# First sort's shares, the loads of the FFN, the choice of tokens, and idle products on TensorE in a graph and feed-forward kernel

## What is computed

```python
x = x + _L0_gnn_ref(_layernorm(x), edge_index, W, a_l, a_r)         # graph attention, 4 heads
x = x + _L0_ffn_ref(_layernorm(x)[None], ...)[0]                    # FFN on the chosen half of the nodes
x = x + _L1_gnn_ref(_layernorm(x), src, dst, edge_type_4, ...)      # 4 relations, mean over dst, relu
x = x + _L1_ffn_ref(_layernorm(x)[None], ...)[0]                    # 8 experts, top 2
```

```python
weights = (jnp.einsum('bsd,do->bso', x, wr) + br)[..., 0]
k = max(1, int(CAPACITY * s)); kk = k - 1        # 1561 of 3125
_, idx = jax.lax.top_k(weights, k); sel_idx = idx[:, :kk]
h = jax.nn.gelu(jnp.einsum('bkd,dh->bkh', sel, w1) + b1)
y = (jnp.einsum('bkh,hd->bkd', h, w2) + b2) * w_sel[..., None]
```

## Time and profile before

| | us |
|---|---|
| median of 3 runs (1991.79 to 1993.94) | 1993.55 |
| profiled execution, whole | 1998.76 |
| its span, first to last instruction | 1997.0 |
| PE busy, DVE busy, POOL busy, ACT busy | 1437.6, 1302.2, 1391.3, 569.5 |
| mean granted clock of PE | 0.85 of 2.4 GHz |

### The profile page before, as it was taken

How to read it: one execution, slowest core, us unless ns; L and a number is a source line. 1 busy time by engine, 2 the same in 40 slices (tenths; PEclk the granted TensorE clock), 3 DMA queues, 4 the chain that set the end, 5 groups by cost and what they waited for, 6 DMA issues and landing times.

```text
span 1997.0 us, 22558 instructions
## 1 busy us (share of the span) xinstructions
PE 1437.6 (72%) x6235; PEld 944.4 (47%) x6235; DVE 1302.2 (65%) x2919; ACT 569.5 (29%) x1670; POOL 1391.3 (70%) x1400
## 2 busy tenths in 40 slices
PE   5666267788888887569999967766666776457980
PEld 3333045665565555447775434333333333256870
DVE  6999477788898887475995035445444444666544
ACT  0687211146566663032332311000000000242220
POOL 0788777777777777778875457777777777546771
PEclk9799678889999999779999979889877777557995
DMA  5111034444444444802003573333333333412337
GB/s 92 12 31 28 6 102 108 108 105 118 119 119 118 119 104 119 107 17 62 1 2 83 142 220 105 105 106 105 105 106 106 105 106 104 46 52 72 102 103 213
DMA packets 105960, 183.76 MB, mean 92 GB/s; under 512 B 31722, under 2 KB 70077, under 8 KB 105714
## 3 DMA queue, kind: packets, MB, share of 16 engines
q0 software_dynamic: 56928, 134.61, 27.9%
q1 hardware_dynamic: 47603, 45.16, 8.6%
q10 hardware_dynamic: 1308, 2.56, 0.5%
HBM read 151.56 MB, written 30.39 MB: 91 GB/s over the span
## 4 chain that ended last, share of the span: by engine, by line
POOL 38%; PE 19%; DVE 17%; issue 15%; DMA 9%; DVEq 1%; ACT 1%; SPq 0%; POOLq 0%; ACTq 0%
POOL gath L891 29%; POOL slot_tab L711 8%; PE ps L925 6%; DMA gath<-y_tab,index_b 4%; PE ps L1314 4%; PE ps L1703 2%; DVE hot L1160 2%; DMA gath<-h_tab,index_a 2%; DVE hot L1163 2%; PE ps L1714 2%; DVE gath L964 1%; DVE acc L916 1%; DMA wide<-y_nodes 1%; DVE junk_d L1116 1%; DVE hot_c L637 1%
## 5 line engine op out<-in xcount | busy, mean ns | idle before, releaser
L925 PE MATMUL ps<-gath,hot 128*125 128x260 f32 (+1 forms) x1808 | 615.5, 476 | 297.6 <-DVE gath L964 108.5
L925 PEld LDWEIGHTS ps<-gath,hot 128*125 128x125 f32 x1808 | 354.8, 222 | 518.0 <-DMA gath<-y_tab,index_b 190.5
L891 POOL DMA_INDIRECT gath<-h_tab,index_a x464 | 447.4, 964 | 141.1 <-issue 136.5
L891 POOL DMA_INDIRECT gath<-y_tab,index_b x440 | 416.1, 946 | 166.9 <-issue 121.5
L916 DVE TENSOR_TENSOR acc<-acc,ps 125x257 f32 (+1 forms) x672 | 284.6, 423 | 330.8 <-PE ps L925 303.7
L666 PE MATMUL ps<-hot_c,pay 125*128 125x440 f16 (+1 forms) x884 | 191.9, 370 | 60.3 <-ACT pay L655 60.3
L711 POOL DMA_INDIRECT slot_tab<-sent_word,sent_to x119 | 150.5, 1265 | 87.7 <-DVE sent_to L473 51.8
L721 POOL DMA_INDIRECT slot_tab_b<-sent_word_b,sent_to_b x136 | 164.7, 1211 | 38.8 <-issue 34.5
L655 ACT ACTIVATE pay<-hot_r,plan_b 125x128 f16<-125x128 f16 x578 | 172.0, 386 | 0.0
L666 PEld LDWEIGHTS ps<-hot_c,pay 125*128 125x128 f16 x884 | 86.2, 101 | 157.3 <-ACT pay L655 77.0
L964 DVE TENSOR_TENSOR gath<-gath,ps 128x1024 f32<-128x1024 f32 x116 | 136.0, 1214 | 0.0
(11 more groups left out here) (330 smaller groups left out, 2033.7 us busy)
## 6 DMA issues: line engine op xcount, KB each, us to landing
y_tab<-ybuf SPq DMA_DIRECT2D x25, 448.0 KB
gath<-h_tab,index_a POOLq DMA_INDIRECT x464, 2.8
gath<-y_tab,index_b POOLq DMA_INDIRECT x440, 2.8
h_tab<-hbuf SPq DMA_DIRECT2D x25, 113.8 KB
xa<-in_x SPq DMA_DIRECT2D x1, 2800.0 KB
xa<-in_x SPq DMA_DIRECT2D x5, 560.0 KB
xn_tab<-acc SPq DMA_DIRECT2D x25, 112.0 KB
out<-xa SPq DMA_DIRECT2D x5, 560.0 KB
```

Source lines behind the costliest of these rows:

```text
L891: p.indirect_dma_start(gath[:, ring(k) + s, 0:width], None, table, bass.IndirectOffsetOnAxis(ap=index[g][:, col:col + 1], axis=0)).then_in ...
L925: ins = t.matmul(ps[0:NP, 4 + q % 2, 0:width], hot[:, s, :], gath[:, s, 0:width], start=(e == 0), stop=(e == n - 1))
```

## The change

Six things, named in the order of the program:

1. A_STEPS is 19 instead of 18, so SENT is 102 instead of 119.
2. In ffn_sync the loads wait for every second group from 18 on: x in groups 18 to 26, w1 in 28 to 34, w2 in 36 to 42. For that w1_s, w2_s, hid, rel_s and w_turned lie elsewhere in SBUF.
3. ffn_vector scales and norms at once, then waits for the weights and takes the dots. The rank counts are gone. The choice is a search over the bits of the float score in CHOICE: 7, 7, 7, 7 and 3 bits, of which each partition tries one value and counts over the whole row; PE sums the partitions' votes. PE does this at eight places of its own order (CHOICE_AT: set, part, block or tile).
4. stay_warm puts products of the identity with itself on PE, whose results nobody reads: 20 before the FFN's turns, one behind each column of the last three relation groups, 3 for each of 15 tiles in routing, 24 and 14 around the placing of nodes.
5. The relation norms (routing) go in two groups, tiles 0 to 14 and 15 to 24, behind all 25 sums; DVE norms the second group itself.
6. ACT loads its gelu table before it waits for the weights.

```diff
-A_STEPS = 18
+A_STEPS = 19
...
+CHOICE = ((7, 24), (7, 17), (7, 10), (7, 3), (3, 0))
+
+CHOICE_AT = ((1, "up", 2), (1, "up", 6), (2, "up", 1), (2, "up", 4), (2, "up", 7), (2, "down", 1), (2, "down", 3), (3, "up", 2))
...
+    def stay_warm(t, n, bank):
+        for _ in range(n):
+            t.matmul(ps[:, bank, 384:512], ident[:, :], ident[:, :], start=True, stop=True, skip_group_check=True)
...
-        s.wait_ge(planned, 2)
+        s.wait_ge(words_ready, 2)
...
+        phase = iter(range(B_PHASE + 2, GROUPS, 2))
+        beside = lambda: s.wait_ge(added["a"], QUADS * next(phase) + 2)
         for i in range(SETS):
-            s.wait_ge(added["a"], QUADS * (B_PHASE + 2 + 5 * i) + 2)
+            beside()
...
-            s.wait_ge(added["a"], QUADS * (B_END + q) + 2)
+            beside()
             s.dma_start(w1_s[:, :, q * D:(q + 1) * D], matrix(w1)[:, :, q * D:(q + 1) * D]).then_inc(ffn_in, 16)
...
-            s.wait_ge(added["a"], QUADS * (B_END + 4 + q) + 2)
+            beside()
             s.dma_start(w2_s[:, 2 * q:2 * q + 2, :], matrix(w2)[:, 2 * q:2 * q + 2, :]).then_inc(ffn_in, 16)
...
-        s.dma_start(w_all[:, :], bcast(w_tab, NP)).then_inc(wall_in, 16)
+        s.dma_start(w_all[:, :], bcast(w_tab, 128)).then_inc(wall_in, 16)
...
+        for r, (bits, low_bit) in enumerate(CHOICE):
+            v.tensor_tensor(tried[:, :], digits[:, r:r + 1], found[:, :], ALU.bitwise_or).then_inc(vector_step, vn.up())
+            step()
+            v.tensor_scalar(junk, w_all[:, :], tried[:, :].bitcast(F32), None, ALU.is_ge, ALU.add, accum_out=votes[:, :]).then_inc(vector_step, vn.up())
+            step()
+            v.tensor_scalar(chosen[:, :], votes[:, :], wanted[:, 0:1], None, ALU.is_ge).then_inc(wcol_ready, 1)
+            v.wait_ge(wcol_turned, 3 + r)
+            v.tensor_scalar(digit[:, :], ps[:, 7, 256 + r:257 + r], -1.0, float(2 ** low_bit), ALU.add, ALU.mult).then_inc(vector_step, vn.up())
...
+    def choose_tensor(t_eng, place):
+        if place not in CHOICE_AT:
+            return
+        n = CHOICE_AT.index(place)
+        t_eng.wait_ge(wcol_ready, n + 1)
...
+        elif n < 2 + len(CHOICE):
+            tries = 2 ** CHOICE[n - 2][0]
+            ins = t_eng.matmul(ps[:, 7, 254 + n:255 + n], ones[0:tries, :], chosen[0:tries, :], start=True, stop=True)
...
+        ins.then_inc(wcol_turned, 1)
...
-        v.wait_ge(ffn_in, FFN_IN)
-        for t in range(U5):
-            dot(t)
         norm_scale(v, 3, rest)
         v.wait_ge(norm_ready, 3)
...
+        for t in range(U5, 2 * U5):
+            norm(t)
+        v.wait_ge(ffn_in, FFN_IN)
         for t in range(NT):
...
+            if t + 2 * U5 < NT:
+                norm(t + 2 * U5)
+            dot(t)
+        choose_vector(v)
...
+        stay_warm(t_eng, 20, 7)
         for t in range(U5):
             turn(t)
...
+                choose_tensor(t_eng, (i, "up", c))
...
+                choose_tensor(t_eng, (i, "down", u))
...
                 sum_unit(t, "b", k, j, D + 1)
+                if k >= GROUPS_B - 3:
+                    stay_warm(t, 1, 7)
...
+    HALVES = (slice(0, 3 * U5), slice(3 * U5, NT))
...
+        for t in range(8, 23):
+            t_eng.wait_ge(x3_made, t + 1)
+            stay_warm(t_eng, 3, 7)
...
+        stay_warm(t_eng, 24, 5)
         t_eng.wait_ge(er_tile, 2)
...
         ins.then_inc(nodes_made, 1)
+        stay_warm(t_eng, 14, 7)
...
+        for t in range(NT):
+            v.scalar_tensor_tensor(flat(xb, t), acc_cols(t, D), s2[:, t:t + 1], flat(xb, t), ALU.mult, ALU.add).then_inc(third_summed, 1)
+        split = HALVES[1].start
+        measure(0, split)
+        v.wait_ge(vector_step, vn.n)
+        norm_sums(v, HALVES[0])
+        measure(split, split + 2)
+        norm_scale(v, 6, HALVES[0])
+        measure(split + 2, NT)
+        v.wait_ge(vector_step, vn.n)
+        norm_sums(v, HALVES[1])
+        norm_scale(v, 7, HALVES[1])
+        v.wait_ge(norm_ready, 7)
+        for t in range(split, NT):
+            v.tensor_scalar(acc_cols(t, D), flat(xa, t), rstd[:, t:t + 1], nmr[:, t:t + 1], ALU.mult, ALU.add).then_inc(late_normed, 1)
```

More of the change, by code:

```diff
@@ L221, in build @@
     junk_d = mid.tile("junk_d", [NP, D])
-    above = mid.tile("above", [NP, NT, 3])
-    junk = hot[0:NP, :, :].rearrange("p s n -> p (s n)").bitcast(BF16)[:, 0:N]
-    same = mid.tile("same", [NP, NP])
+    digits = mid.tile("digits", [128, len(CHOICE)], I32)
+    found, tried, digit = (mid.tile(n, [128, 1], I32) for n in ("found", "tried", "digit"))
+    votes, chosen, positive, sign, wanted, limit = (mid.tile(n, [128, 1]) for n in ("votes", "chosen", "positive", "sign", "wanted", "limit"))
+    over, level, run = (mid.tile(n, [NP, NT]) for n in ("over", "level", "run"))
+    junk = hot[:, :, :].rearrange("p s n -> p (s n)").bitcast(BF16)[:, 0:N]
     dinv = mid.tile("dinv", [NP, NT, HEADS])
@@ L1456, in keep_turned, with root @@
-        def keep_turned(i):
-            for t in range(i * U5, (i + 1) * U5):
-                a.wait_ge(x_turned, TURN["moe"] + t + 1)
-                if t >= U5:
-                    a.wait_ge(logit_made, t - U5 + 1)
-                a.copy(xt[:, t % U5, :, :], route_turn(t).rearrange("p (k n) -> p k n", k=2)).then_inc(xt_copied, 1)
-        a.activation(first_root[:, :], ones[0:1, 0:1], ACT.Sqrt)
-        for i in range(AHEAD):
-            relu(i)
-        for i in range(SETS):
-            normed(i)
-            if i + AHEAD < SETS:
-                relu(i + AHEAD)
-            keep_turned(i)
+        def root(h):
+            a.wait_ge(var_ready, 6 + h)
+            a.activation(tmp25[:, HALVES[h]], var[:, HALVES[h]], ACT.Sqrt).then_inc(root_done, 1)
@@ new lines, in keep_turned @@
+        def keep_turned(t):
+            a.wait_ge(x_turned, TURN["moe"] + t + 1)
+            if t >= U5:
+                a.wait_ge(logit_made, t - U5 + 1)
+            a.copy(xt[:, t % U5, :, :], route_turn(t).rearrange("p (k n) -> p k n", k=2)).then_inc(xt_copied, 1)
+        a.activation(first_root[:, :], ones[0:1, 0:1], ACT.Sqrt)
+        for t in range(NT):
+            a.wait_ge(third_summed, t + 1)
+            a.activation(flat(xb, t), flat(xb, t), ACT.Relu).then_inc(third_relu, 1)
+        root(0)
@@ L1471, in route_scalar @@
+        a.wait_ge(norm_ready, 6)
+        for step in range(NT + 2):
+            t = step
+            if t < HALVES[1].start:
+                a.activation(acc_cols(t, D), flat(xa, t), ACT.Identity, bias=nmr[:, t:t + 1], scale=rstd[:, t:t + 1]).then_inc(x_normed, 1)
+            if step == U5:
+                root(1)
+            t = step - 2
+            if t >= 0:
+                keep_turned(t)
         a.wait_ge(logit_ready, 1)
@@ L1528, in route_vector, with measure @@
         v.wait_ge(self_added, NT)
-        def third(i):
-            for t in range(i * U5, (i + 1) * U5):
-                v.scalar_tensor_tensor(flat(xb, t), acc_cols(t, D), s2[:, t:t + 1], flat(xb, t), ALU.mult, ALU.add).then_inc(third_summed, 1)
-        for i in range(AHEAD):
-            third(i)
-        for i in range(SETS):
-            for t in range(i * U5, (i + 1) * U5):
+        def measure(lo, hi):
+            for t in range(lo, hi):
                 v.wait_ge(x3_made, t + 1)
```

133 lines of the change are left out of this document (74 added, 59 removed).

## The result

The changed kernel takes 1973.31 us (median of 4 runs, 1971.69 to 1973.74) where the kernel before takes 1993.55 (four runs): ratio 0.9896, 95% interval 0.9883 to 0.9908, 20.2 us less. The forecast was 1970.7, 22.9 less. Its profiled execution took 1971.69 us, span 1969.7, so the two profiles differ by 27.3 us, 7 more than the medians.

| from, to | before | changed | gained | forecast |
|---|---|---|---|---|
| start, first gather | 249.07 | 231.94 | 17.1 | 14.3 |
| first gather, DVE's last wait of attention | 601.25 | 597.73 | 3.5 | 1.5 |
| that wait, PE's first FFN turn | 17.90 | 18.02 | -0.1 | |
| first turn, last down product's end | 195.68 | 188.04 | 7.6 | 6.1 |
| that end, first sum of routing | 658.89 | 658.43 | 0.5 | 0 |

The account below looks back on a forecast made before the run. POOL's gather issue was taken as the bound, so gains come only before, between and behind the two runs: 14.3 + 1.5 + 6.1 + 0 + 0 + 1.0 = 22.9 us, median 1970.7 us, range 1958 to 1979.

Parts of the forecast that it names:

- Part 1: First sort: one step more and 17 words fewer start the gathers 14.3 us sooner, ends 12 and 15.5.
- Part 2: End of the first gather run: padding sets most of the late landing; moving the loads gains 1.5 us, ends 0 and 11.0.
- Part 3: FFN: ends at 1057.3 instead of 1063.9; less 0.5 for two narrow margins, 6.1 us gained, ends -1 and 9.
- (a): FFN start: 20 idle products fill 8.6 to 10.4 us of PE's 8.71 gap; set 0's ups take 17.04, not 18.95.
- (d): FFN choice: row of scores, 19.53 us after the turn, counted by 954.9, just when PE asks; PE's 3.16 us wait goes.
- Part 4: Last three relation groups: idle products change 0 us, since late landings set the pace; ends 0.5 gained, 3 lost.
- Part 5: Routing: norms in two groups gain 0 us, with the clock falling after some eight tiles; ends -3.5 and +5.
- C: Rival, chance 0.05: the moved loads stall the first gather run, 20 us less gain, 1990.7.
- E: Rival, chance 0.12: the weights were the whole lateness at the first gather run's end, 9.5 us more gain, 1961.2.
- D: Rival, chance 0.20: routing keeps 2.4 GHz, 5 us more gain, 1965.7.
- A: Rival, chance 0.03: identity products never raise PE's clock and make it late in each place; 6.6 us lost, 2000.
- B: Rival, chance 0.17: in the FFN PE waits at more of the eight places, 6 us less gain, 1976.7.

Follow-up runs that it names:

- part 1 alone: The kernel before with only A_STEPS 19 instead of 18: 2230.61 us against 2252.16 for before on the same chip, ratio 0.9902.
- the 75 products: The changed kernel with 5 idle products instead of 3 per routing tile: 2233.69 us, ratio 0.9914 to before; routing 56.83 us, 0.8 less.

## Why the prediction was right, point by point

- **Part 1** has the mechanism right and the size too small: 17.1 us for 14.3, above my upper end of 15.5. I took DVE's step at its duration beside a sending POOL (8.7), and left PE's close 2.57 behind DVE's last one-hot, which ends at 227.56 now; it starts 1.63 behind it. POOL's maximum was done at 223.05, hidden by more than the 2.7 forecast.
- **Part 2**: the reading that the padding columns set the late landing is shown, by the share of 0.93 without weights and by the run with spread rows. The weights' 1.5 us measured 0.4, which is not told apart from nothing. Of the 3.5 in the table 2.0 are before's own scatter: its repeat has 599.29 us for this stretch, the changed kernel with 18 steps 598.96. With loads early or late the time is equal, where the cover's lack would have cost 20 us. The rule of the Trainium skill that loads interleave with gathers on the same 16 engines ("DMA: Bandwidth & Descriptors", "Issuing engines are not separate DMA queues") is not contradicted; it cost nothing here.
- **Part 3**: (a) failed. A record of an identity product takes 0.116 us at 2.4 GHz; I had taken 0.214 to 0.26 from the experts' products, which ran slowly there (2.08 us for eight, 1.16 where idle products lead up to them). So PE idled and set 0 gained nothing. The end of set 0 by (b), the wait by (c) and the end of the FFN by (d) came out to 0.1, 0.9 and 1 us. But (d) had the row of scores wrong: it was there 9.5 us behind DVE's copy, not 19.5, and DVE had its first votes over the row by 922.8, where PE asked at 933.6. The margin that I gave as a tenth of a us was 10.8, which changed nothing in the sum. The failure of (a) cost only some 0.7, because DVE is next in line: it normed tile 5 21.5 us behind the first turn, and PE asked 22.1 behind it. 7.6 us were gained against a before that had stopped; against the one profile that had not (part 1 alone, on another chip), 2.6.
- **Part 4**: 0.5 us in the table, my upper end, but not told apart from nothing: this stretch takes 658.89 and 658.18 us in the two profiles of before, 658.43, 657.19 and 657.04 in three of the changed kernel (as it is, with late loads, with 18 steps). **Part 5**: -1.7, inside its ends. The turn came 28.0 us behind the first sum (forecast 28.7) and the tiles were as slow as my bound "held at 0.50"; that the clock should rise first failed for the same wrong record. **Part 6**: 0.4 for 1.0. The first eight products are 0.8 shorter, but from them to the end it is 180.70 and 181.22 us before and 180.3 to 181.3 in four changed kernels of that chip, so the total shows nothing.
- **Rivals**: C and E fell with the late loads, D with the 75 products. A is excluded by the last three relation groups, where a unit that nothing held took 1.3 to 1.4 us at 1.2 GHz, not 2.0, and the clock rose. B did not happen: PE waits at one of the eight places. What I gave for B, the margin of a tenth in (d), was the misread row.
- **The sum** is right by a margin that owes something to luck: by the profiles 27.3, by the medians 20.2. By the medians part 1 gave 15.6 where 14.3 were forecast, and the other five together 3.8 (2.4 to 6.4) where 8.6 were: the one error covers a part of the other. The difference between profiles and medians lies in before, whose single runs span 7 us, the changed kernel's 2. One cause that reaches 5.3 us is seen in the profiles, the stop behind the rank counts. That it is what scatters before's timed runs was not shown.

## What to carry to other kernels

Look at what padding reads: 128 reads of one row made a gathered column land in 1.8 us where POOL issues one in 1.25, and that set the end of both gather runs until each partition got a row of its own (on the chips with pauses the DMA share fell as well, but the time at the end did not). When a stretch is shortened, check who else has to be done by its end; here POOL's 16 small transfers and the silence behind them ate 8 of 14 us won. And price idle products from a row of the same product: they hold PE's clock only if they reach to the work itself, and what they save is kept only if PE is what comes last there.

## What was not expected of the hardware

- TensorE's clock stays at 1.2 GHz while PE's records cover 5.00 of 5 us for over 20 us, under 125-column turns and 8-column products, even with a 128-column float32 product per tile between them. Where these tiles began at 2.4 GHz it fell shortly behind a wait of PE for ACT (1.45 and 0.87 us). 38 such products that reached to the work kept the clock, and the 64 up products behind ran at 2.4 GHz. "TensorE: Matmul & The Clock Gate", "What's actually happening" (the Trainium skill), has activity release the throttle; in these tiles busy records did not.
- POOL is silent for 5.5 to 7.1 us, where it waits for nobody else, ahead of its first maximum over partitions and ahead of its first addition of two tensors (5.61 and 6.99 in two runs above). Both stand behind a string of indirect transfers, but it is not the change of kind that costs: later ones cost 0.2, and behind the 440 relation gathers POOL goes on at once, with a kind that it had used at the program's start:

```profile
1683.09 0.94 POOL L911 DMA_INDIRECT gath<-y_tab,index_b  x1 [0.30 <-issue]
1684.04 0.51 POOL L1504 IOTA order<- 125x200 f32 x1
```

  The Trainium skill ("GPSIMD Engine Reference", "2.1 Instruction dispatch") gives about 6 us for loading the code of a function that is called first. That fits the places and the size of both silences; the trace shows no load.
- 20 float32 products of 128x128 took 4.63 us at 2.4 GHz, two records each.
- On three of four chips the engines pause together for 1 to 2 us, dozens of times, under gathers, and every kernel takes 13% longer; the change was worth the same there (0.9907 to 0.9896).
